# Four roundings moved ahead of the last diagonal, and one output product moved ahead of the turning of the gates

## The chip, the cores and the metric

The kernel runs on one core of a Trainium2 chip. The metric is the device time of one execution in microseconds (us). Three runs of the kernel before gave a median of 1544.88 us, from 1544.23 to 1545.69.

## The reference

A transformer layer in float32 on x of 2 x 2048 x 512 (4096 tokens): causal attention with 16 heads of 32 and rotary positions, and then a feed-forward layer with eight low-rank experts of which each token takes two. Cut to what matters:

```
def attention(x, Wq, Wk, Wv, Wo):            # x is the layernorm of the input
    q, k = rope(heads(x @ Wq.T)), rope(heads(x @ Wk.T))
    v = heads(x @ Wv.T)
    scores = where(causal, q @ k.T / sqrt(32), -inf)
    return merge(softmax(scores) @ v) @ Wo.T

def ffn(x, base_w, base_b, router_w, router_b, lora_A, lora_B):
    result = x @ base_w.T + base_b
    probs = softmax(x @ router_w.T + router_b)
    gate = top-2 of probs, made to sum to 1, zero elsewhere     # n x 8
    mid = einsum('nd,edr->ner', x, lora_A) * gate[:, :, None]
    return result + 2.0 * einsum('ner,erd->nd', mid, lora_B)

x = x + attention(layernorm(x), ...)
x = x + ffn(layernorm(x), ...)
```

## The kernel before, in words

There are three stages, each written out for every engine in its own order: `project` (queries, keys and values, with rope, into DRAM scratch), `attend` (attention) and `finish` (the output projection `Wo`, the second layernorm and the experts). An operand of a matmul is split in two: its rounded part ("hi", a cast) and the rest ("lo", the operand less its rounded part, a subtraction). A product is then hi x hi + hi x lo + lo x hi, twelve matmuls of 512 columns for one block of 128 tokens by 512.

`attend` works through 8 groups of 4 heads. In a group the four tiles of 512 queries (t = 0 to 3) take 4, 8, 12 and 16 steps, one for each 128 keys: 40 steps, done as 20 pairs, numbered 0 to 19. The last tile is pairs 12 to 19, and pairs 18 and 19 are its diagonal. For each pair TensorE (PE) makes the scores (L1014), ScalarE (ACT) the exponentials (L1114), PE the values (L1027). The sum of the exponentials is formed by adding the two steps of a pair elementwise and multiplying the result with ones on PE. In most pairs of a tile the added pair is not multiplied at once: it goes into the tile `a_gather` (two halves), either directly, or into `a_pair` and from there by an accumulating DMA of 1024 KB that GpSimd (POOL) issues (`join`, L860). Below, "join 14" is the DMA of pair 14; in the last tile pairs 14 and 16 join half 0 and pairs 15 and 17 join half 1. PE multiplies half 0 in `sums` of pair 18 and half 1 in `sums` of pair 19 (L1049), each behind a wait on all the joins of that half. Then come the later of the two steps' own columns (L1053) and `a_pair` (L1057).

`a_pair` has two places, for even and odd pairs. `wait_place_of_pair` keeps an addition from overwriting a place that a join still reads: pair 16 waits for join 14, 17 for 15, 18 for 16, and 19 for 17. ACT in turn starts a pair's exponentials only when the addition two pairs before is done.

In the last group the pairs from NO_ITEMS = 10 on are special. Row maxima (`item_max`) are over, and VectorE (DVE) does the additions (`add_pair`, L1171), which POOL does otherwise; POOL is left with the joins and with zeroing the later keys on the diagonal (`drop_later_keys`, L944). DVE also prepares the stage after it (`split_early`): the four parts of `Wo` are split (n = 0 to 3, L1156 and L1158, 128 x 512 each, from `shared` into `a_third` and `a_k_stack0`), and the first context, 128 x 2048 in `f_ctx` (`cin`), into `a_k_first` (n = 4). SP loads `f_ctx` at pair 10 (L894). When its split is done (`c_lo_done`), SP loads the second context, 1024 KB, into the same tile (L922); its next instructions are four small loads of router weights (L198), and then a wait for the last `sums`.

`finish` walks over eight tiles of 512 tokens. PE starts it with `attention_out` (L1375) for the first tile, four products, and two of the second tile, and then turns the normalised x. Its order in a tile T is in `tile`: router, down, turning of the logits, (for T > 0 two output products of the next tile,) two base products (L1435), turning of the gates (L1440), one output product of the next tile, the experts' products of two blocks (L1450), and so on. The turning waits for DVE's chain of small gate operations (`gates`, to L1633). Behind it DVE multiplies (`gate_mid`, L1638), ACT rounds (L1530), DVE subtracts (`mid_rest`, L1642), and only then can L1450 start.

The lines that set where DVE splits, and the order on PE:

```
SPLIT_FROM = NPAIR - 7
...
                    if last and p >= NO_ITEMS:
                        add_pair(g, p)
                    if last and SPLIT_FROM <= p <= SPLIT_FROM + KT:
                        split_early(p - SPLIT_FROM)
...
                base(T, u, 1)
                turn_gates(T)
                attention_out(T + 1, 1 - u, 2)
                experts(T, 0)
```

The functions that the change touches, and what calls them:

## Time and profile before

| what | value |
|---|---|
| median of 3 runs | 1544.88 us |
| the profiled execution | 1543.78 us, its span 1542.0 us |
| granted TensorE clock, mean | 0.998 |
| PE busy | 1512.4 us, 98% |
| DVE, ACT, POOL busy | 1134.3, 755.7, 890.7 us |
| HBM read and written | 96.23 and 58.72 MB |

Times in the rows are counted from the start of the span. Busy PE time is modelled, since matmuls are pipelined; starts are what is compared here. In a timeline row stand start, duration, engine, line, operation, tiles and count, and in brackets how long the engine had been idle and what released it. The chain that ended last follows the work back from the end to what released each step.

### The profile page before, as it was taken

What the parts mean: (1) busy time and instruction counts of PE and PEld (TensorE: products, weight loads), DVE (VectorE), ACT (ScalarE), POOL (GpSimd) and SP (SyncE); (2) the same over time, 40 slices, a digit from 0 to 9 for tenths busy, and PEclk for the clock granted to TensorE, in tenths of its full rate; (3) what the DMA queues carried; (4) which work ended last, traced back from release to release, by engine and by line L of the source; (5) the groups of instructions that cost most, each with busy time, mean ns of one, the idle gap of its engine ahead of it and who ended that gap; (6) DMA issues with size and microseconds to landing.
All of it is one profiled execution on the core that took longest, in us unless ns stands there. A gap on an engine that the chain in (4) does not pass through costs nothing.

```text
span 1542.0 us, 24788 instructions
## 1 busy us (share of the span) xinstructions
PE 1512.4 (98%) x9056; PEld 979.6 (64%) x9056; DVE 1134.3 (74%) x2277; ACT 755.7 (49%) x1540; POOL 890.7 (58%) x597
## 2 busy tenths in 40 slices
PE   6999999999999999999999999999999989999999
PEld 5888887745555555555555555555555537777777
DVE  6766666887877777777777877777787777666665
ACT  3222222145656656666666666665675673223221
POOL 2333232446778788788887887788887821121111
PEclk9999999999999999999999999999999999999999
DMA  6656685883476377368369359449445364222311
GB/s 205 211 188 208 204 261 188 227 189 67 90 167 149 84 158 165 84 144 186 84 138 192 83 117 203 93 97 207 99 95 127 86 145 138 82 83 95 139 67 55
DMA packets 120403, 215.83 MB, mean 140 GB/s; under 512 B 12504, under 2 KB 45784, under 8 KB 113112
## 3 DMA queue, kind: packets, MB, share of 16 engines
q1 hardware_dynamic: 102384, 136.20, 32.8%
q0 software_dynamic: 8064, 58.72, 18.6%
q10 hardware_dynamic: 9840, 19.40, 3.5%
q8 instruction: 69, 1.13, 0.3%
q14 instruction: 46, 0.38, 0.1%
HBM read 96.23 MB, written 58.72 MB: 100 GB/s over the span
## 4 chain that ended last, share of the span: by engine, by line
PE 89%; DVE 5%; DMA 3%; SPq 1%; issue 1%; ACT 1%; POOL 0%; DVEq 0%; POOLq 0%; ACTq 0%
PE a_st L1014 16%; PE a_mx L260 16%; PE a_av L1027 16%; PE p_pair L518 11%; PE f_wo_ps L1375 6%; PE f_out_ps L1435 5%; PE p_v L530 5%; PE a_sum L260 3%; PE a_sum L1049 2%; DVE a_part L275 2%; PE a_sum L1057 2%; PE f_out_ps L1450 1%; PE f_mid_ps L1375 1%; DMA a_third<-a_neg_rows 1%; PE f_tr_ps L1394 1%; DMA a_gather<-a_pair 1%
## 5 line engine op out<-in xcount | busy, mean ns | idle before, releaser
L1114 ACT ACTIVATE a_probs<-a_st 128x512 f32<-128x512 f32 (+2 forms) x1244 | 573.3, 547 | 353.9 <-PE a_st L1014 348.2
L275 DVE TENSOR_REDUCE a_part<-a_mx 128x1 f32<-128x512 f32 (+2 forms) x773 | 495.3, 681 | 90.5 <-PE a_mx L260 79.3
L963 POOL TENSOR_TENSOR a_pair<-a_probs 128x1024 f32<-128x1024 f32 (+2 forms) x224 | 401.9, 1835 | 29.8 <-issue 14.7
L963 POOL TENSOR_TENSOR a_gather<-a_probs 128x1024 f32<-128x1024 f32 x76 | 179.9, 2388 | 87.9 <-ACT a_probs L1114 87.9
L392 POOL TENSOR_TENSOR p_rot<-p_mul 128x1024 f32<-128x1024 f32 x32 | 87.5, 2735 | 193.5 <-DVE p_mul L696 193.5
L1368 POOL TENSOR_TENSOR f_x<-f_x,f_bias 128x512 f32<-128x512 f32 x32 | 40.2, 1286 | 200.2 <-DVE f_xn L1588 200.2
L1027 PE MATMUL a_av<-a_probs,shared 128*32 128x512 f32 (+3 forms) x1280 | 142.7, 546 | 0.0
L1027 PE MATMUL a_av<-a_probs,a_v 128*32 128x512 f32 (+3 forms) x1280 | 139.8, 537 | 2.2 <-POOL a_probs L944 2.2
L278 DVE CUSTOM_DVE_ANT_0 a_mx<-a_mx,f_ctx 128x512 f32<-128x512 f32 (+1 forms) x155 | 94.7, 630 | 51.4 <-PE a_mx L260 51.4
L944 POOL TENSOR_SCALAR_AFFINE_SELECT a_probs<-a_probs 128x512 f32<-128x512 f32 x128 | 88.6, 756 | 61.2 <-ACT a_probs L1114 57.3
L1014 PE MATMUL a_st<-a_q_stack,a_k_stack 98*128 98x512 f32 (+3 forms) x287 | 101.4, 371 | 1.0 <-DMA a_q_stack<-a_neg_rows 1.0
L260 PE MATMUL a_mx<-a_k_stack,a_q_stack 96*128 96x512 f32 (+3 forms) x252 | 88.0, 380 | 0.1
L604 ACT ACTIVATE p_rot_hi<-p_rot 128x1024 fp32r<-128x1024 f32 x32 | 34.0, 1061 | 110.2 <-POOL p_rot L392 94.4
L278 DVE CUSTOM_DVE_ANT_0 a_sum<-a_sum,f_ctx 128x512 f32<-128x512 f32 (+1 forms) x85 | 53.8, 633 | 29.6 <-PE a_sum L260 27.9
L700 DVE TENSOR_TENSOR p_rot_lo<-p_rot,p_rot_hi 128x1024 fp32r<-128x1024 f32 x28 | 45.7, 1633 | 36.8 <-ACT p_rot_hi L604 36.8
L518 PE MATMUL p_pair<-p_xt_lo,p_w_hi 128*128 128x512 f32 x256 | 69.9, 394 | 0.0
L1014 PE MATMUL a_st<-a_third,a_k_stack 98*128 98x512 f32 (+3 forms) x189 | 69.6, 380 | 0.1
L860 POOL DMA_DIRECT2D a_gather<-a_pair x56 | 49.2, 879 | 34.1 <-DVE a_pair L1171 18.4
L695 DVE TENSOR_TENSOR p_mul<-p_pair,p_tab 128x1024 f32<-128x1024 f32 x32 | 39.1, 1220 | 39.7 <-PE p_pair L518 39.7
L1027 PEld LDWEIGHTS a_av<-a_probs,shared 128*32 128x32 f32 x1280 | 30.5, 109 | 57.2 <-issue 42.2
L1027 PEld LDWEIGHTS a_av<-a_probs,a_v 128*32 128x32 f32 x1280 | 30.3, 108 | 57.1 <-issue 39.6
L1014 PEld LDWEIGHTS a_st<-a_q_stack,a_k_stack 98*128 98x128 f32 x287 | 54.0, 189 | 18.9 <-ACT a_probs L1114 9.7
(241 smaller groups left out, 3037.7 us busy)
## 6 DMA issues: line engine op xcount, KB each, us to landing
a_gather<-a_pair POOLq DMA_DIRECT2D x56, 1024.0 KB, 7.2
qk_scratch<-p_rot_hi SPq DMA_DIRECT2D x32, 512.0 KB, 3.1
qk_scratch<-p_rot_lo SPq DMA_DIRECT2D x32, 512.0 KB, 3.9
a_k_stack<-qk_scratch SPq DMA_DIRECT2D x60, 256.0 KB, 8.2
a_q_first<-qk_scratch SPq DMA_DIRECT2D x48, 256.0 KB, 6.9
a_third<-qk_scratch SPq DMA_DIRECT2D x36, 256.0 KB, 5.5
v_scratch<-p_v_st SPq DMA_DIRECT2D x32, 256.0 KB, 7.1
ctx_scratch<-a_ctx_st SPq DMA_DIRECT2D x32, 256.0 KB, 3.1
```

The source lines that it names most:

```text
L260: mm = pe.matmul(places[:, i, :], queries[0:96, head, qi * P:(qi + 1) * P], keys[0:96, head, 0:width], start=(i == 0), stop=not masked_her ...
L275: dve.tensor_reduce(found, scores.rearrange("p (h n) -> p h n", n=width), AX.X, ALU.max).then_inc(self.max_done, 1)
L278: dve.tensor_tensor_reduce(out=scores, in0=scores, in1=self.mask[:, TT - width:TT], scale=1.0, scalar=3.0 * MASKED, op0=ALU.add, op1=ALU.m ...
L392: pool.tensor_tensor(rot[:, par], mul[:, par, :, 0, :], mul[:, par, :, 1, :], ALU.add).then_inc(rot_done, 1)
L518: mm = pe.matmul(pair_ps[p % 2][:, half, :], w[:, kt, cols], a[u][:, kt, :], start=(n == 0), stop=(n == len(passes) - 1))
L530: mm = pe.matmul(v_ps[s % 2][:, :], a[u][:, kt, s * P:(s + 1) * P], w[:, kt, 2 * DM:3 * DM], start=(n == 0), stop=(n == len(passes) - 1))
L944: pool.affine_select(block, block, pattern=[[0, HG], [1, P]], compare_op=ALU.is_ge, fill=0.0, base=0, channel_multiplier=-1).then_inc(mask ...
L963: pool.tensor_tensor(place[:, h:h + 2, q0:TT], probs[:, s % RING, h:h + 2, q0:TT], probs[:, (s + 1) % RING, h:h + 2, q0:TT], ALU.add).then ...
L1014: pe.matmul(score_bank(g, n)[:, q0:TT], block, queries[t][0:98, h, q0:TT], start=True, stop=True).then_inc(st_done, 1)
L1027: mm = pe.matmul(av_ps[h * DK:(h + 1) * DK, q0:TT], vb[par][:, j, h * DK:(h + 1) * DK], probs[:, s % RING, h, q0:TT], start=j == 0, stop=s ...
L1114: act.activation(probs[:, s % RING, h, q0:TT], score_bank(g, HG * s + h)[:, q0:TT], ACT.Exp, scale=SCORE_SCALE).then_inc(exp_done, 1)
L1375: mm = pe.matmul(out, w, a, start=(n == 0), stop=(n == len(pairs) - 1))
```

## The change

Two edits. In the last group of `attend` the splits start at pair 10 instead of 13, and the first context is split in four parts of 128 x 512 instead of one of 128 x 2048. The parts of `Wo` go behind the additions of pairs 10 to 13, the parts of the context behind those of pairs 13 to 16, so pair 13 has two. The parts count on semaphores of their own, and behind the last part DVE waits for all four and then raises `c_hi_done` and `c_lo_done`, as the one split did. In `finish`, for the first tile only, the output product (1, block 2) stands ahead of the turning of the gates instead of behind it.

```
-SPLIT_FROM = NPAIR - 7
...
+                    m = n - KT
                     dve.wait_ge(early.ctx_loaded, 16)
-                    raw, hi, lo = early.cin, early.c_hi, early.c_lo
-                    hi_done, lo_done, count = early.c_hi_done, early.c_lo_done, 1
+                    raw, hi, lo = early.cin[:, m, :], early.c_hi[:, m, :], early.c_lo[:, m, :]
+                    hi_done, lo_done, count = early.c_part_done, early.c_rest_done, m + 1
                 dve.tensor_copy(hi, raw).then_inc(hi_done, 1)
                 dve.wait_ge(hi_done, count)
                 dve.tensor_tensor(lo, raw, hi.bitcast(F32), ALU.subtract).then_inc(lo_done, 1)
+                if n == 2 * KT - 1:
+                    dve.wait_ge(early.c_rest_done, KT)
+                    dve.sem_inc(early.c_hi_done, 1)
+                    dve.sem_inc(early.c_lo_done, 1)
...
-                    if last and SPLIT_FROM <= p <= SPLIT_FROM + KT:
-                        split_early(p - SPLIT_FROM)
+                    if last and NO_ITEMS <= p < NO_ITEMS + KT:
+                        split_early(p - NO_ITEMS)
+                    if last and NO_ITEMS + KT - 1 <= p < NO_ITEMS + 2 * KT - 1:
+                        split_early(p - NO_ITEMS + 1)
...
                 base(T, u, 1)
+                if T == 0:
+                    attention_out(1, 1, 2)
                 turn_gates(T)
-                attention_out(T + 1, 1 - u, 2)
+                if T > 0:
+                    attention_out(T + 1, 1 - u, 2)
                 experts(T, 0)
```

DVE's order in the last group before, from the addition of pair 13 (the first row) to that of pair 18 (the last). `a_third` and `a_k_stack` take the parts of `Wo`, `a_k_first` the context; L1171 is an addition.

```order
L1171 TENSOR_TENSOR a_gather<-a_probs 128x1024 x2
L1156 CAST a_third<-shared 128x512
L1158 TENSOR_TENSOR a_k_stack<-shared,a_third 128x512
L1171 TENSOR_TENSOR a_pair<-a_probs 128x1024 x2
...
L1156 CAST a_third<-shared 128x512
L1158 TENSOR_TENSOR a_k_stack<-shared,a_third 128x512
L1171 TENSOR_TENSOR a_pair<-a_probs 128x1024 x2
L1156 CAST a_k_first<-f_ctx 128x2048
L1158 TENSOR_TENSOR a_k_first<-f_ctx,a_k_first 128x2048
L1171 TENSOR_TENSOR a_pair<-a_probs 128x2x384 x2
```

Now the same stretch, from the third part of `Wo` behind the addition of pair 12 on; L1175 is the addition, and the first L1175 row is pair 13.

```order
L1156 CAST a_third<-shared 128x512
L1158 TENSOR_TENSOR a_k_stack<-shared,a_third 128x512
L1131 STREAM_TRANSPOSE a_sum_t<-a_sum 128x512
L1135 RECIPROCAL a_rsum<-a_sum_t 128x16
L1140 STREAM_TRANSPOSE a_rsum_b<-a_rsum 128x512
L1175 TENSOR_TENSOR a_gather<-a_probs 128x1024 x2
L1156 CAST a_third<-shared 128x512
L1158 TENSOR_TENSOR a_k_stack<-shared,a_third 128x512
L1156 CAST a_k_first<-f_ctx 128x512
L1158 TENSOR_TENSOR a_k_first<-f_ctx,a_k_first 128x512
L1175 TENSOR_TENSOR a_pair<-a_probs 128x1024 x2
L1156 CAST a_k_first<-f_ctx 128x512
```

A split now stands ahead of the turning of tile 2's sums, which comes before the addition of pair 13, and two splits instead of one stand between the additions of pairs 13 and 14. At the other end nothing stands any more between the additions of pairs 17 and 18:

```order
L1158 TENSOR_TENSOR a_k_first<-f_ctx,a_k_first 128x512
L1175 TENSOR_TENSOR a_pair<-a_probs 128x1024 x2
L1156 CAST a_k_first<-f_ctx 128x512
L1158 TENSOR_TENSOR a_k_first<-f_ctx,a_k_first 128x512
L1175 TENSOR_TENSOR a_pair<-a_probs 128x1024 x2
L1175 TENSOR_TENSOR a_pair<-a_probs 128x2x384 x2
```

The last context part is behind the addition of pair 16 (second row), so `c_lo_done` rises ahead of the addition of pair 17 (fifth row), and SP's load of the second context with it.

PE in the first tile of `finish` before: base products, the turning of the gates, the output product, the experts' products.

```order
L1435 MATMUL f_out_ps<-f_base_lo,f_xt_hi 128x512 x4
L1435 MATMUL f_out_ps<-f_base_hi,f_xt_lo 128x512 x4
L1440 MATMUL f_lg_ps<-f_ident,f_gate_x 128x128 x4
L1375 MATMUL f_wo_ps<-a_third,a_q_first 128x512 x4
L1375 MATMUL f_wo_ps<-a_k_stack,a_q_first 128x512 x4
L1375 MATMUL f_wo_ps<-a_third,a_q_first 128x512 x4
L1450 MATMUL f_out_ps<-f_b_hi,f_mt_hi 128x512
```

And now, at the same place:

```order
L1443 MATMUL f_out_ps<-f_base_lo,f_xt_hi 128x512 x4
L1443 MATMUL f_out_ps<-f_base_hi,f_xt_lo 128x512 x4
L1383 MATMUL f_wo_ps<-a_third,a_q_first 128x512 x4
L1383 MATMUL f_wo_ps<-a_k_stack,a_q_first 128x512 x4
L1383 MATMUL f_wo_ps<-a_third,a_q_first 128x512 x4
L1448 MATMUL f_lg_ps<-f_ident,f_gate_x 128x128 x4
L1458 MATMUL f_out_ps<-f_b_hi,f_mt_hi 128x512
```

The twelve matmuls of the product have changed places with the four of the turning, and nothing stands any more between the turning and the first of the experts' products.

## Rows read from the trace of the kernel before

**Rows 1.** The page: the chain that ended last, by engine.
```profile
PE 89%; DVE 5%; DMA 3%; SPq 1%; issue 1%; ACT 1%; POOL 0%; DVEq 0%; POOLq 0%; ACTq 0%
```

**Rows 2.** The chain that ended last: start us, us, what.
```profile
1251.63 2.37 DVE a_pair L1171 x2
...
1254.29 8.28 DMA a_gather<-a_pair
```

**Rows 3.** Timeline of DVE, end of the last group: start us, us, engine, line.
```profile
1242.11 0.71 DVE L1141 STREAM_TRANSPOSE a_rsum_b<-a_rsum 128x512 f32<-128x512 f32 x1
1243.28 3.19 DVE L1171 TENSOR_TENSOR a_gather<-a_probs 128x1024 f32<-128x1024 f32 x2 [0.47 <-ACT a_probs L1114]
1246.40 0.41 DVE L1156 CAST a_third<-shared 128x512 fp32r<-128x512 f32 x1
...
1247.46 2.35 DVE L1171 TENSOR_TENSOR a_pair<-a_probs 128x1024 f32<-128x1024 f32 x2
...
1257.02 2.36 DVE L1171 TENSOR_TENSOR a_pair<-a_probs 128x1024 f32<-128x1024 f32 x2 [1.97 <-DMA a_gather<-a_pair]
...
1262.60 2.36 DVE L1171 TENSOR_TENSOR a_pair<-a_probs 128x1024 f32<-128x1024 f32 x2 [2.15 <-DMA a_gather<-a_pair]
1264.87 1.22 DVE L1156 CAST a_k_first<-f_ctx 128x2048 fp32r<-128x2048 f32 x1
...
1269.54 2.68 DVE L1171 TENSOR_TENSOR a_pair<-a_probs 128x768 f32<-128x768 f32 x2
1273.39 0.76 DVE L1171 TENSOR_TENSOR a_pair<-a_probs 128x256 f32<-128x256 f32 x2 [1.17 <-issue]
```

**Rows 4.** POOL: join 17 and the first masks of the diagonal.
```profile
1265.25 0.97 POOL L860 DMA_DIRECT2D a_gather<-a_pair  x1 [4.71 <-DVE a_pair L1171]
...
1266.22 1.24 POOL L944 TENSOR_SCALAR_AFFINE_SELECT a_probs<-a_probs 128x512 f32<-128x512 f32 x2
```

**Rows 5.** Line L860: landing of joins 14, 17, and one beside key loads.
```profile
DMA to landing us min/median/max: 6.9/6.9/6.9
...
DMA to landing us min/median/max: 8.1/8.1/8.1
...
DMA to landing us min/median/max: 9.9/9.9/9.9
...
DMA to landing us min/median/max: 6.8/7.2/11.0
```

**Rows 6.** Windows: busy us by engine, granted clock, DMA share, GB/s.
```profile
592.60:602.50 9.90, 9.90 (x77) 5.38 (x76) 7.18 (x13) 4.67 (x14) 8.14 (x8) 1.00 1.01 222
...
1251.00:1273.40 22.40, 18.30 (x144) 8.04 (x140) 16.38 (x15) 15.16 (x36) 7.69 (x7) 1.00 0.98 206
...
1264.00:1268.00 4.00, 1.76 (x17) 0.72 (x13) 3.97 (x3) 1.40 (x5) 2.56 (x4) 1.00 0.92 190
```

**Rows 7.** Timeline of PE, end of the last group.
```profile
1272.27 0.85 PE L1057 MATMUL a_sum<-a_pair,a_ones 128*32 128x384 f32 x8 [1.82 <-DVE a_pair L1171]
...
1273.59 1.04 PE L1049 MATMUL a_sum<-a_gather,a_ones 128*32 128x512 f32 x8
...
1275.00 1.21 PE L1375 MATMUL f_wo_ps<-a_third,a_k_first 128*128 128x512 f32 x4
```

**Rows 8.** SP: the load of the second context.
```profile
1269.64 0.37 SPq L922 DMA_DIRECT2D f_ctx<-ctx_scratch  x1
```

**Rows 9.** Timeline of PE, first tile of the last stage.
```profile
1304.09 1.10 PE L1435 MATMUL f_out_ps<-f_base_hi,f_xt_lo 128*128 128x512 f32 x4
1306.33 0.66 PE L1440 MATMUL f_lg_ps<-f_ident,f_gate_x 128*128 128x128 f32 x4 [1.15 <-DVE f_gate_x L1633]
...
1309.60 0.40 PE L1450 MATMUL f_out_ps<-f_b_hi,f_mt_hi 128*128 128x512 f32 x1
```

**Rows 10.** Timeline of DVE there.
```profile
1308.41 0.69 DVE L1642 TENSOR_TENSOR f_mt_lo<-f_gated_mid,f_mt_hi 128x512 fp32r<-128x512 f32 x1 [0.70 <-ACT f_mt_hi L1530]
```

**Rows 11.** The chain that ended last: the output product there.
```profile
1306.98 2.78 PE f_wo_ps L1375 x12
```

More of the change, by code:

```diff
@@ L1237, in __init__ @@
         self.c_lo_done = ctx.enter_context(nc.semaphore("f_c_lo_done"))
+        self.c_part_done = ctx.enter_context(nc.semaphore("f_c_part_done"))
+        self.c_rest_done = ctx.enter_context(nc.semaphore("f_c_rest_done"))
     def place(self):
```

## The prediction

> **What bounds the kernel now.** I read the chain by engine first [rows 1]: 89% of the span is PE, so a change off PE's path moves the time only where PE waits. Both edits stand at such places, and each is judged by PE's start behind it.
>
> The first place is the end of the last group. The timeline of PE [rows 7] shows `sums` of pair 18 waiting 1.82 us for DVE's addition, then `sums` of pair 19 (L1049) at 1273.59, and `finish` at 1275.00. DVE's timeline [rows 3] shows why the addition of pair 18 was late: the whole-context split stands from 1264.87 to 1269.54. That is the stall the new order takes away. But the reader should also see the two additions before it, at 1257.02 and 1262.60, which had waited 1.97 and 2.15 us for a DMA, and the last one, at 1273.39, after 1.17 us of idle put down to "issue". The code says what that one waits for: its place, read by join 17. Join 17 was issued at 1265.25 and landed 8.1 us later [rows 4, 5], at 1273.35. The addition began 0.04 us behind it, and L1049 of pair 19, which waits for the same join, 0.24 us behind it. So two things end this stage within 0.3 us of each other: DVE's late addition, and a row of joins.
>
> That row is a chain. The addition of pair 14 frees join 14, its landing (6.9 us, [rows 5]) the addition of pair 16, which gives join 16; the chain of waits shows the other half of it: addition of pair 15, then 8.28 us of join 15 [rows 2], then the addition of pair 17 and join 17. And the four share the same DMA engines: from 1251.0 to 1273.4 their share was 0.98 [rows 6], 206 GB/s, 4.6 MB, of which the four joins are 4.2 MB. They queue behind each other, some 5.5 us each, so a later join 14 is a later join 17.
>
> The second place is the first tile of `finish`. PE is idle 1.15 us before the turning of the gates at 1306.33 [rows 9], waiting for DVE. Behind the turning stands the output product, 2.78 us [rows 11], and the experts' products start at 1309.60 without a wait.
>
> **First edit: the splits.** The span's end moves with L1049 of pair 19, so the cost is that of join 17's landing.
>
> Removed: 4.67 us of DVE between the additions of pairs 17 and 18 (1264.87 to 1269.54, [rows 3]). Alone this would bring PE's L1057 of pair 18 forward by at most about 2 us, since the masks it also needs end at 1266.22 + 1.24 = 1267.46 [rows 4]. But L1049 of pair 19 can't start before 1273.35. Worth: 1273.59 - 1273.35 = 0.24 us at most.
>
> Added: the splits go ahead of the chain of joins. One split of 128 x 512 takes 1.06 us from start to the next start (1246.40 to 1247.46, [rows 3]); a context part has the same shape and tile types. Those of pairs 10 and 11 fall into idle time of DVE; I give them zero. That of pair 12 delays the turning back, which ended at 1242.11 + 0.71 = 1242.82, to 1243.88; the addition of pair 13 began at 1243.28 after 0.47 us of idle, so it loses 0.60. Behind pair 13 stand two splits in place of one: another 1.06. The addition of pair 14 starts 1.66 us later, say 1.7, and its row of before has no idle time ahead of it to soak that up. It ends join 14's wait, so joins 14 to 17 shift by 1.7 each: the waits of pairs 16 and 17 for a DMA (1.97 and 2.15 us) are waits for these very joins, so they are no slack. The context parts behind the additions of 14, 15 and 16 do fit into those waits (each 1.06 against 1.97 or more); behind 14 the addition of pair 15 starts about 1.2 later, which only keeps pace. Join 17 shifts to 1275.05 by this alone. Bounds: 1.0 (if POOL's slowing of the addition of pair 13, 3.19 us for two against 2.35, falls away) and 2.2.
>
> Moved: SP's load of the second context. Before, it was issued at 1269.64 [rows 8], when join 17 was nearly through. Now `c_lo_done` rises behind the addition of pair 16: 1257.02 + 1.7 + 2.36 + 1.06 = 1262.1. Join 16 has then just been issued and join 17 hasn't. All of the load's 1.05 MB passes ahead of or among the last two joins; the small router loads behind it come along. Nobody needs that data early: PE's first use of the second context lies behind four products. What it costs: a join issued at 592.6 landed after 9.9 us instead of 6.9, and in its time 222 GB/s x 9.9 us = 2.2 MB moved, 1.15 MB of it not its own [rows 5, 6]. That is 3.0 us for 1.15 MB, 2.6 us for each. In the window of before 4.6 - 4.2 = 0.4 MB of other traffic was already inside; so 0.65 MB are new, 1.7 us. Bounds: 0, if the load only takes gaps, and 3.4, from the slowest join of all, 11.0 - 6.9 = 4.1 us [rows 5], less the 0.7 that a load in join 17's way could have cost already. I take 1.7, by the row nearest in bytes.
>
> The Trainium skill speaks against the edit here too: "DMA: Bandwidth & Descriptors", section "Issuing engines are not separate DMA queues", says that transfers started by different engines run on the same 16 DMA engines and interleave. By that rule the load isn't free though SP issues it and POOL the joins; the 9.9 us of the join at 592.6 [rows 5] agree, and a reading by separate queues would put this term at 0.
>
> Sum of the first edit: join 17 lands at 1273.35 + 1.7 + 1.7 = 1276.75. L1049 of pair 19 starts at 1276.8 instead of 1273.59: **+3.2 us**. The late addition of pair 18 no longer shows: with masks and join 16 shifted it ends near 1273. The addition of pair 19 takes 0.76 and is done before PE reaches it, as before.
>
> **Second edit: the product ahead of the turning.** Counts don't change; twelve matmuls change places with four. PE's idle time ends at 1306.33 and was 1.15, so the base products ended at 1305.18 [rows 9]. Now the output product runs from there, 2.78 us, to 1307.96, and the turning starts 1.6 us later than before, though the gates were ready. By starts, four matmuls of 512 take 0.93, which puts the end of the base products at 1304.09 + 0.93 = 1305.02 and the shift at 1.5. What follows the turning is a chain over three engines, DVE, ACT, DVE, which ended at 1308.41 + 0.69 = 1309.10 [rows 10]: 2.8 us behind the turning's start. Before it lay beside the output product (which ended at 1309.60, 0.5 later), now beside nothing. The experts' products start at 1309.15 + 1.5 = 1310.65 instead of 1309.60: **+1.1 us**. The idle 1.15 us is filled, and about 2.3 us open behind the turning. Bounds: +0.7 if PE resumes sooner behind the subtraction, +1.4. Downstream each step (the additions, normalising, the next turning) hangs on this product's successors and moves along.
>
> **Sum.** +3.2 + 1.1 = +4.3 us: the profiled execution goes from 1543.78 to 1548.1; its own time lies 1.1 under the median, so the median goes from 1544.88 to 1549.2. Between `finish`'s start and the gates nothing gives time back: PE's products run in one piece there.
>
> **Rivals.**
> 1. *The load is free.* Its packets only fill gaps. For: the joins alone move about 200 GB/s, far from what loads reach. Against: the DMA share is 0.98 [rows 6]. Then +1.7 - 0.2 + 1.1 = +2.6: 1547.5.
> 2. *The joins don't carry the delay* (the other side: not slower by what can be told). If the DMA queue weren't what sets join 17, a later join 14 would be made good within the waits of pairs 16 and 17 (1.97 and 2.15 us), join 17 would land at 1273.35 or before, and L1057 of pair 18 would come up to 2.0 us sooner. It decides from the point where join 17 is not the last: all 2.0 us would reach the end if the 1.17 us of "issue" weren't its landing but DVE's own. With the second edit's +1.1 that is -0.9 at best, 1544.0, and +0.9, 1545.8, if L1049 stays. For: the view names no releaser. Against: 0.04 us between landing and start.
> 3. *The load weighs more*, because its packets and the router's all go before join 17: +3.4 in place of 1.7, +6.0 in all, 1550.9.
> 4. *PE's clock drops.* With longer stalls PE is idle for much of 1265 to 1277. In the four us from 1264 PE was busy 1.76 at a granted clock of 1.00, the upper level [rows 6], so stalls of this size didn't lower it; a product at the lower level would take twice its 2.78: up to +2.8 more, 1552.
>
> **How the numbers follow.** The forecast with its own spread has 0.55, rival 1 0.17, rival 2 0.13, rival 3 0.11, rival 4 0.04. A measurement of this kernel tells about 0.2%, 3.1 us, from no change. Over that lie 0.50 of the forecast's 0.55 (+4.3), 0.03 of rival 1 (+2.6), and rivals 3 and 4: slower 0.68. Faster by as much would need more than rival 2's best case; I give it 0.03 for what I may have overlooked, and same the other 0.29. Range: 1546.2 to 1551.4, which leaves out rivals 2 and 4 and the ends of the rest, some 2 in 10.
>
> **What would show each step.** Right: the addition of pair 14 about 1.7 us later relative to the exponentials; the second context issued 7 us earlier, near 1262; joins 16 and 17 landing after 9 us or more; PE's last wait of the stage now at L1049 of pair 19 behind a DMA, over 2 us, and the wait at L1057 of pair 18 changed into one for masks or join 16; in `finish` no wait before the turning and one of about 2.3 us before the first experts' product. Wrong: join 17 landing within 8 us of its issue with no shift of its issue, or L1049 following the values without a gap. The forecast falls if `finish` starts less than 2 us later than before, counted from the last row maximum of the group.

## The result and the profile after

The changed kernel takes 1554.12 us (median of 8 runs, 1548.06 to 1558.48), the kernel before in runs beside it 1543.91 us (8 runs, 1541.15 to 1547.81): ratio 1.0066, 95% interval 1.0046 to 1.0085. It is 10.2 us slower where +4.3 was forecast, and its 1554.1 lies 2.7 us above the range. The direction was right, the size wrong. One execution of the kernel before (1803.67 us) and one of `best` (2379.20 us) among the experiments were in a far slower state and are left out of every ratio, mean and fit below.

The profiled execution took 1555.68 us (span 1553.9, mean granted clock 0.992; before 1542.0 and 0.998). The page's chain by engine, which answers to [rows 1]:

```profile
PE 92%; DVE 4%; DMA 2%; issue 1%; ACT 1%; SPq 0%; POOL 0%; POOLq 0%; DVEq 0%; ACTq 0%
```

This page doesn't name the cause: DMA even lost a percent. It is in the last group. Timeline of DVE there (columns as in [rows 3]):

```profile
1250.63 2.35 DVE L1175 TENSOR_TENSOR a_pair<-a_probs 128x1024 f32<-128x1024 f32 x2
...
1260.17 2.36 DVE L1175 TENSOR_TENSOR a_pair<-a_probs 128x1024 f32<-128x1024 f32 x2 [2.79 <-DMA a_gather<-a_pair]
...
1266.72 2.36 DVE L1175 TENSOR_TENSOR a_pair<-a_probs 128x1024 f32<-128x1024 f32 x2 [3.13 <-DMA a_gather<-a_pair]
1272.20 1.83 DVE L1175 TENSOR_TENSOR a_pair<-a_probs 128x768 f32<-128x768 f32 x2 [3.11 <-POOL a_probs L943]
1281.01 0.76 DVE L1175 TENSOR_TENSOR a_pair<-a_probs 128x256 f32<-128x256 f32 x2 [6.99 <-DMA a_gather<-a_pair]
```

These are the additions of pairs 14, 16, 17, 18 and 19. The split is gone from between pairs 17 and 18, and the addition of pair 18 now waits for POOL's masks; but that of pair 19 waits 6.99 us for a DMA. In the timelines of POOL and SP, join 17 is issued at 1269.38 and the load of the second context at 1263.78, 5.6 us ahead of it (before, 4.4 us behind join 17: [rows 4, 8]). The first row is join 16:

```profile
1262.83 0.86 POOL L859 DMA_DIRECT2D a_gather<-a_pair  x1 [5.34 <-DVE a_pair L1175]
1269.38 0.86 POOL L859 DMA_DIRECT2D a_gather<-a_pair  x1 [5.69 <-DVE a_pair L1175]
```

```profile
1263.78 0.37 SPq L921 DMA_DIRECT2D f_ctx<-ctx_scratch  x1
```

Landing of join 17, from the view of its line; [rows 5] had 8.1:

```profile
  DVE a_pair L1175: 7.0, 1
  PEld a_sum L1048: 3.9, 1
  PE a_sum L1048: 3.6, 1
...
DMA to landing us min/median/max: 11.6/11.6/11.6
```

PE, in answer to [rows 7]:

```profile
1270.95 1.25 PE L1026 MATMUL a_av<-a_probs,a_v 128*32 128x512 f32 x8 [4.23 <-POOL a_probs L943]
...
1280.97 1.06 PE L1048 MATMUL a_sum<-a_gather,a_ones 128*32 128x512 f32 x8 [3.64 <-DMA a_gather<-a_pair]
...
1282.79 1.65 PE L1383 MATMUL f_wo_ps<-a_third,a_k_first 128*128 128x512 f32 x3
```

The wait of 1.82 us ahead of L1057 of pair 18 is gone. PE now waits 4.23 us for POOL's masks, which stand behind join 17's issue on POOL (before, 2.24 us for the same masks), and the last sums of the group wait 3.64 us for join 17. `finish` starts at 1282.79. Behind it, the place of the second edit; compare [rows 9]:

```profile
1316.76 0.60 PE L1448 MATMUL f_lg_ps<-f_ident,f_gate_x 128*128 128x128 f32 x4
1319.53 0.80 PE L1458 MATMUL f_out_ps<-f_b_hi,f_mt_hi 128*128 128x512 f32 x1 [2.17 <-DVE f_mt_lo L1653]
...
1325.35 1.08 PE L1443 MATMUL f_out_ps<-f_base_hi,f_xt_hi 128*128 128x512 f32 x4
```

The 1.15 us of idle ahead of the turning are gone, and 2.17 us stand behind it. The windows (columns as in [rows 6]) show what [rows 6] didn't have, a granted clock below 1.00 from 1270 to 1290:

```profile
1253.29:1280.98 27.69, 19.38 (x141) 8.66 (x138) 11.60 (x14) 16.74 (x36) 6.12 (x8) 0.94 0.88 191
...
1270.00:1280.00 10.00, 6.39 (x60) 2.63 (x60) 1.83 (x2) 3.69 (x8) 2.91 (x5) 0.83 0.82 197
1280.00:1290.00 10.00, 9.03 (x50) 6.70 (x51) 5.28 (x8) 0.51 (x4) 2.11 (x5) 0.83 0.48 159
```

To compare kernels I count times in the group from the start of its transposition of the negated row maxima on DVE ("the group's zero": 1228.56 before, 1229.94 after), which lies ahead of both edits. A landing is the issue plus a time given in tenths, so differences of landings are good to about 0.1 us:

| | before | after | difference |
|---|---|---|---|
| the group's zero, from the span's start | 1228.56 | 1229.94 | +1.38 |
| addition of pair 14 starts | 18.90 | 20.69 | +1.79 |
| join 17 issued | 36.69 | 39.44 | +2.75 |
| join 17 landed | 44.79 | 51.04 | +6.25 |
| first product of `finish` | 46.44 | 52.85 | +6.41 |
| first experts' product | 81.04 | 89.59 | +8.55 |
| end of the span, from the span's start | 1542.0 | 1553.9 | +11.9 |

The forecast had +3.2 in the fifth line (first product of `finish`) and +4.3 in the sixth (first experts' product).

### The profile page after: what moved, and what is told of

Same layout as the page of the kernel before. It is cut to its first block, busy times and chain, and to the rows that moved or that the text cites. A ratio compares the mean times of both kernels' runs of the same rounds, so it can differ in the third digit from the quotient of the medians.

```text
span 1553.9 us, 24796 instructions
## 1 busy us (share of the span) xinstructions
PE 1520.4 (98%) x9056; PEld 985.3 (63%) x9056; DVE 1133.3 (73%) x2283; ACT 756.3 (49%) x1540; POOL 889.4 (57%) x597
## 3 DMA queue, kind: packets, MB, share of 16 engines
q8 instruction: 69, 1.13, 0.3%
## 4 chain that ended last, share of the span: by engine, by line
PE 92%; DVE 4%; DMA 2%; issue 1%; ACT 1%; SPq 0%; POOL 0%; POOLq 0%; DVEq 0%; ACTq 0%
PE a_mx L259 17%; PE a_st L1013 16%; PE a_av L1026 16%; PE p_pair L517 11%; PE f_wo_ps L1383 6%; PE p_v L529 5%; PE f_out_ps L1443 5%; PE a_sum L259 3%; PE a_sum L1048 2%; PE a_sum L1056 2%; DVE a_part L274 2%; PE f_mid_ps L1383 1%; DMA a_gather<-a_pair 1%; PE f_out_ps L1458 1%; PE f_lg_ps L1413 1%; PE a_mx L263 1%
```

## The experiments

Twelve kernels were run, four at a time, with the kernel before beside each lot; its medians there were 1544.75, 1544.23 and 1544.98 us, and each ratio is to the lot's own. All runs of the first edit below but `best` and the repeat have `finish` as before. They were to tell apart what makes join 17 late (the later join 14, the early load, the split's place) and how much is left for the second edit and the clock.

### Each edit alone

`first_only` is the first edit with `finish` as before; `second_only` is this alone:

```
+                if T == 0:
+                    attention_out(1, 1, 2)
                 turn_gates(T)
-                attention_out(T + 1, 1 - u, 2)
+                if T > 0:
+                    attention_out(T + 1, 1 - u, 2)
```

Expected of `first_only`:

> The first edit alone (splits from pair 10, context in four parts), the output product of the first tile left behind the turning of the gates. Measured from the last row maximum of the group to the first product of the last stage, the changed kernel needed 6.4 us more than the kernel before. Theory of the joins (the splits ahead of the addition of pair 14 delay join 14, and the second context's load runs among joins 16 and 17): this stretch is again about 6.4 longer, and the median 6.5 to 8 us over the kernel before, the part over 6.4 being products at the lower clock behind the stall. Rival, that the second edit made most of the loss (its own wait of 2.2 us and the low clock behind it): under 4 us over.

Measured: 1551.85 us, ratio 1.0041 [1.0026, 1.0057]. The last sums start at 50.96 behind the group's zero, as in the kernel with both edits (51.03), and `finish` 5.96 us later than before. The theory of the joins holds, and the rival (under 4 us over) is out.

Expected of `second_only`:

> The second edit alone. By the order of the instructions: 1.0 us later from the turning of the logits to the first of the experts' products. In the changed kernel the clock was also low behind that wait, and the products there took 1.6 us more. Theory that the new wait of 2.2 us alone brings the clock down: 2.6 us over, a granted clock under 1.00 in the 12 us behind it. Rival, that the low clock there came from the first edit's stalls as well: 1.0 us over and the clock at 1.00.

Measured: 1547.36 us, ratio 1.0013 [1.0000, 1.0025]. The timeline of PE:

```profile
1297.90 1.20 PE L1435 MATMUL f_out_ps<-f_base_hi,f_xt_hi 128*128 128x512 f32 x4
...
1306.38 0.60 PE L1440 MATMUL f_lg_ps<-f_ident,f_gate_x 128*128 128x128 f32 x4
1309.14 0.50 PE L1450 MATMUL f_out_ps<-f_b_hi,f_mt_hi 128*128 128x512 f32 x1 [2.17 <-DVE f_mt_lo L1645]
```

From the first base product to the first experts' product it is 1309.14 - 1297.90 = 11.24 us, and 11.24 in the changed kernel too (1308.29 to 1319.53); before it was 10.28. The second edit costs 0.96 us by order, the same with and without the first, and 1.07 up to the next base product (15.53 against 14.46 us from the first one). The granted clock behind the wait stayed at 1.00, as the rival had it, so that wait alone didn't bring the clock down. The first edit is the larger part.

### The load held back, splits as in the change

`first_held` takes the two semaphores' rise away from behind the last split and puts it behind the addition of pair 17; `first_held19` puts it behind that of pair 19 (shown):

```
-                if n == 2 * KT - 1:
-                    dve.wait_ge(early.c_rest_done, KT)
-                    dve.sem_inc(early.c_hi_done, 1)
-                    dve.sem_inc(early.c_lo_done, 1)
...
                         add_pair(g, p)
+                    if last and p == NPAIR - 1:
+                        dve.wait_ge(early.c_rest_done, KT)
+                        dve.sem_inc(early.c_hi_done, 1)
+                        dve.sem_inc(early.c_lo_done, 1)
```

> As the first edit alone, but DVE raises the two context semaphores behind the addition of pair 17 instead of with the last part, so SP issues the second context's load where it did before; the splits still stand ahead of join 14. Theory that the early load is the larger term: join 17 lands 2 to 3 us later than in the kernel before (relative to the last row maximum), the stretch to the last stage is 2 to 3 us longer, the median 2 to 3.5 over. Rival, that the delay of the additions alone does it (join 15 issued too close behind join 14): the stretch is 5 us longer or more with the load held too.

Measured: 1553.41 us, 1.0056 [1.0034, 1.0077]. It didn't hold the load as meant: SP issued it at 36.99, while the addition of pair 17 was still running, 2.5 us before join 17's issue at 39.48. Join 17 landed at 51.08, no better than in the change (51.04). So an issue 3 us later doesn't help; only one behind join 17's could. Neither theory was tested, since the load hadn't been held. That called for the second version.

> The first edit with its own placement of the splits, and the context semaphores raised behind pair 19, so that only the delay of the additions is left. Theory of the chain (join 14 is issued 1.8 us later, join 17 2.8 later): join 17 lands 2 to 3 us later than before, near 47.3, the last stage starts 2 to 3 us later. Rival, that the joins make the delay good in the waits of pairs 16 and 17: within 0.5 us.

Measured: 1546.75 us, 1.0025 [1.0012, 1.0038]. The load is issued at 46.81, and join 17 lands at 46.51 after 7.0 us:

```profile
DMA to landing us min/median/max: 7.0/7.0/7.0
```

That is 1.72 later than before (44.79), less than the 2 to 3 expected. What is left to delay it is the place of the splits, by which the addition of pair 14 starts at 20.74 instead of 18.90. The forecast's first term was 1.7, but the steps differ: join 17 was issued 2.82 us later (39.51 against 36.69) and landed after 7.0 us instead of 8.1, so the agreement to the tenth is in part luck.

PE shows something else here. Its last sums start at 47.82 behind the group's zero, 1.3 us after join 17's landing and without a wait:

```profile
1271.75 1.20 PE L1048 MATMUL a_sum<-a_gather,a_ones 128*32 128x512 f32 x8
...
1274.29 1.03 PE L1048 MATMUL a_sum<-a_gather,a_ones 128*32 128x512 f32 x8
```

PE came late because the masks and with them the values of pair 18 were late (41.09 against 38.37), and because the granted clock from 1260 to 1270 was 0.76. `finish` starts at 49.22, 2.78 later than before.

### The splits in idle time, the load early, held, and at its old place

Here parts 0 and 1 of `Wo` go behind the addition of pair 10 and parts 2 and 3 behind that of pair 11, where DVE idles; the context's parts behind those of pairs 13 to 16:

```
-                    if last and NO_ITEMS <= p < NO_ITEMS + KT:
-                        split_early(p - NO_ITEMS)
+                    if last and NO_ITEMS <= p < NO_ITEMS + 2:
+                        split_early(2 * (p - NO_ITEMS))
+                        split_early(2 * (p - NO_ITEMS) + 1)
```

`idle_early` raises the semaphores behind the last split as the change does, the three others behind the addition of pair 17, 18 or 19. The addition of pair 14 starts at 18.87 in `idle_early`, as before (18.90), so that the delay of join 14 is out in all four, and the load, with the four small loads behind it, is what differs.

> The first edit with its splits put where DVE was idle: Wo parts 0 and 1 behind the addition of pair 10, 2 and 3 behind pair 11, the context's four parts behind pairs 13 to 16, so that the addition of pair 14 starts as early as in the kernel before; the second context's load stays early (behind pair 16). Theory that the early load is the larger term: joins 16 and 17 land after 9 us or more, and the stretch is 3 to 4.5 us longer. Rival, that the delay of the additions does it: within 1 us of the kernel before.

> The same placement in idle time, and the two context semaphores raised behind the addition of pair 17, so neither the additions nor the load move. Both theories: join 17 lands as in the kernel before or up to 0.5 us sooner, L1057 of pair 18 no longer waits 1.8 us, and the stretch is 0 to 0.5 us shorter, since join 17 sets its end; the median within 1 us of the kernel before. If instead DVE's late addition of pair 18 was the true end of the stage, and join 17 not, it is 1.5 to 2 us shorter.

> The splits in DVE's idle time, as in the two kernels before it, but the two context semaphores raised behind the addition of pair 19, which itself waits for join 17. (Behind pair 17 they were raised while that addition ran, so the second context's load had moved up by 7 us all the same.) The load now can't run beside any join. Theory that the load made joins 16 and 17 late (9.7 and 12.3 us, 4.2 us for join 17): join 17 lands 44 to 45 us behind the last row maximum's transpose, as before or up to 0.7 sooner, and the last stage starts 46 to 46.5 behind it (before: 46.4); the median within 1 us of the kernel before. Rival, that the missing split between pairs 17 and 18 or POOL's earlier masks slow the joins: join 17 lands at 48 or later again.

| | load issued | join 17 issued | join 17 landed | time us | ratio |
|---|---|---|---|---|---|
| before | 41.08 | 36.69 | 44.79 | | |
| `idle_early` | 32.01 | 36.80 | 49.30 | 1550.56 | 1.0038 [1.0023, 1.0052] |
| `idle_held` | 34.17 | 36.67 | 48.97 | 1550.91 | 1.0041 [1.0027, 1.0054] |
| `idle_held19` | 45.12 | 36.77 | 44.77 | 1546.39 | 1.0009 [0.9997, 1.0022] |

The windows from join 14's issue to join 17's landing, first `idle_held19`, then `idle_early`, give the price:

```profile
1252.26:1275.44 23.18, 19.59 (x153) 8.45 (x152) 12.13 (x14) 16.66 (x38) 6.09 (x8) 1.00 0.88 182
```

```profile
1250.25:1278.03 27.78, 21.15 (x154) 8.91 (x154) 11.71 (x14) 18.58 (x39) 5.96 (x8) 0.94 0.89 190
```

23.18 us x 182 GB/s = 4.2 MB, the four joins alone. 27.78 x 190 = 5.3 MB, the joins and the load. So 1.06 MB more go with 4.6 us more, 4.3 us per MB; the joins' own bytes take 23.18 / 4.2 = 5.5 there. The same stretch of the kernel before (1250.11 to 1273.35) moved 198 GB/s in 23.24 us, 4.6 MB. So 0.4 MB of the load went through behind join 17's issue for nothing, at a higher rate than `idle_early` reached: where the bytes stand counts, and not only how many they are.

`idle_held` missed: it was meant to leave the load where it was, but the load went out at 34.17 and join 17 landed at 48.97 instead of at 44.8. `idle_held19` is the run that both theories needed. Join 17 lands at 44.77 there, as the load theory had it; its rival, 48 or later through POOL's earlier masks or the missing split, is out. The waits of PE, of `idle_early` and `idle_held19`:

```profile
1278.02 1.81 PE L1048 MATMUL a_sum<-a_gather,a_ones 128*32 128x512 f32 x8 [4.23 <-DMA a_gather<-a_pair]
```

```profile
1275.54 1.06 PE L1048 MATMUL a_sum<-a_gather,a_ones 128*32 128x512 f32 x8 [1.09 <-DMA a_gather<-a_pair]
...
1286.25 1.20 PE L1384 MATMUL f_wo_ps<-a_third,a_k_first 128*128 128x512 f32 x4 [0.66 <-DVE f_x L1582]
```

The second row of `idle_held19` shows that a load behind everything isn't free either: `x` and the biases stand behind it on SP's queue, `finish` waits for `x` (0.66 and 0.37 us in two places), and the turning of the gates comes 33.3 us behind `finish`'s first product instead of 31.3. The kernel before had the load where it costs neither.

`idle_held18` tests this: the rise behind the addition of pair 18, the load at about its old place.

> Same placement of the splits, but the two semaphores are raised behind the addition of pair 18, so that SP issues the second context at about 41 as in the kernel before: the first edit's removal of the stall, with no delay of join 14 and no early load. Theory A (join 17 sets the end of the group): join 17 lands at 44.8, the last sums start at 44.9 to 45.0 and the first product of the last stage at 46.3, 0.0 to 0.2 before its place in the kernel before, and nothing is lost later, since the load isn't later than before; ratio 0.999 to 1.0005. Rival (the late addition of pair 18 also cost something that shows only in the time): 0.998 or less, 3 us faster.

Measured: 1543.36 us, 0.9998 [0.9987, 1.0009]. The load is issued at 40.16, join 17 lands at 44.97, and PE's rows are

```profile
1272.31 1.07 PE L1048 MATMUL a_sum<-a_gather,a_ones 128*32 128x512 f32 x8 [0.28 <-DMA a_gather<-a_pair]
...
1273.74 0.50 PE L1384 MATMUL f_wo_ps<-a_third,a_k_first 128*128 128x512 f32 x1
```

at 45.00 and 46.43 behind the group's zero; before, 45.03 and 46.44. The stall of 4.67 us on DVE is wholly gone and the end of the stage hasn't moved by more than 0.03 us. Whatever held DVE there, join 17 held PE. The rival, 3 us faster, is out.

### The small loads behind the context

Four router loads (128 x 8 each, 4 KB) go out right behind the context. `router_late` is `idle_early` with these moved:

```
+            sp.wait_ge(early.pair_done, PAIRS_DONE)
             for n in range(W_RING, 2 * W_RING):
                 weights.load(sp, n)
-            sp.wait_ge(early.pair_done, PAIRS_DONE)
```

> Splits in DVE's idle time, the second context issued early (about 32 us behind the start of the group's last transposition), as in the kernel before it with this placement, but the four small router loads (128 x 8 each) that stood right behind it on SP's queue are moved behind SP's wait for the last sums. Theory A, the 1.05 MB of the context itself is what joins 16 and 17 pay for: join 17 lands at 48.8 to 49.4 as with the router loads beside it (49.30), ratio to before 1.003 to 1.005. Theory B, the small packets of the router loads cost the joins part of it: join 17 lands at 47.5 or earlier (44.8 + 1.7 to 2.7), ratio 1.002 or less.

Measured: join 17 lands at 49.04 after 12.2 us; in `idle_early` at 49.30 after 12.5. The small loads cost about 0.3 us of it, and theory A stands on position. The time, 1553.51 us, 1.0047 [1.0027, 1.0067], isn't lower, and `finish` shows why: the load of `x` now queues behind the router's, and PE waits 2.04 us for it (0.17 in `idle_early`):

```profile
1295.44 1.58 PE L1384 MATMUL f_wo_ps<-a_third,a_q_first 128*128 128x512 f32 x4 [2.04 <-DVE f_x L1582]
```

### Both places filled in `finish`

`both_fill` keeps the idle time ahead of the turning filled and puts the next product into the one that opens behind it:

```
+                if T == 0:
+                    attention_out(1, 1, 2)
                 turn_gates(T)
-                attention_out(T + 1, 1 - u, 2)
+                if T == 0:
+                    attention_out(1, 1, 3)
+                else:
+                    attention_out(T + 1, 1 - u, 2)
                 experts(T, 0)
                 experts(T, 1)
-                attention_out(T + 1, 1 - u, 3)
+                if T > 0:
+                    attention_out(T + 1, 1 - u, 3)
```

> The kernel before, but in the first tile the output product (1, block 2) stands ahead of the turning of the gates and the product (1, block 3) behind it, where block 2 stood. Both waits are then filled: PE's 1.15 us ahead of the turning is gone and the chain DVE, ACT, DVE behind it lies beside a product again. Theory: 1.0 us less than the kernel before from the turning of the logits to the second base product of the tile, and no clock change. Rival: block 3's bank or DVE's order (its addition of block 2 comes behind the gating) makes a base product wait as long, and nothing is gained.

Measured: 1543.81 us, 0.9998 [0.9987, 1.0010]. Neither wait is left in PE's rows; from the turning on the rows join end to start:

```profile
1308.05 0.60 PE L1440 MATMUL f_lg_ps<-f_ident,f_gate_x 128*128 128x128 f32 x4
1308.40 1.17 PE L1375 MATMUL f_wo_ps<-a_third,a_q_first 128*128 128x512 f32 x4
...
1311.26 0.40 PE L1450 MATMUL f_out_ps<-f_b_hi,f_mt_hi 128*128 128x512 f32 x1
```

From the first base product to the base product behind the experts' it is 13.33 us, against 14.46 before: 1.13 by position, as expected. The times alone can't tell it from nothing. `best` joins `idle_held18` and `both_fill`:

> The kernel before with its two changes in the form that the runs so far point to: splits in idle time with the load at its old place, and in the first tile the product of block 2 ahead of the turning and that of block 3 behind it. Theory: about 0.2 us from the first and 0.8 to 1.1 us from the second, 1 us in all, ratio 0.9993, which a measurement of this kernel can hardly tell from no change. Rival: the gain in position is given back to the granted clock, ratio 1.000 to 1.001.

Measured: 1543.32 us, 0.9992 [0.9979, 1.0006]. It isn't shown to be faster than the kernel before; its median is 11 us below that of the change.

### The change again, and the clock

> The changed kernel once more, on the chip and beside the runs of the kernel before that the experiments have. Eight runs of it had a mean granted clock of 0.990 to 0.998, mean 0.9934, against 0.9958 over 35 runs of the kernel before; in each kernel a run with the clock 0.001 lower is about 0.9 us longer. Theory A (the lower clock is a consequence of the longer waits at the end): mean clock again 0.993 to 0.994, time 1553 to 1555, ratio 1.0055 to 1.007. Theory B (the clock differed by chance or by chip): mean clock 0.995 to 0.996, time 1551 to 1552.3, ratio 1.0045 to 1.005, which is the parts' sum of order alone, about +7.

Measured: 1554.97 us (6 runs, 1552.79 to 1556.89), 1.0072 [1.0055, 1.0088]; mean granted clock 0.9915. The slower time and the lower clock both come again, the clock even below theory A's 0.993 to 0.994; theory B's 0.995 to 0.996 isn't met. The profiled execution, span 1551.0, has join 17 at 51.09 behind the group's zero, as the first profile (51.04), but its first experts' product at 87.93, 1.66 earlier than there (89.59). Its slow stretch lies in the wait for join 17, where a slow PE costs nothing:

```profile
1270.00:1280.00 10.00, 7.28 (x60) 2.75 (x60) 1.83 (x2) 2.98 (x9) 3.45 (x5) 0.67 0.89 207
1280.00:1290.00 10.00, 8.72 (x56) 6.61 (x57) 6.54 (x13) 1.52 (x5) 2.12 (x5) 1.00 0.47 160
```

The clock isn't the longer waits' alone, though. `second_only`, whose last group is that of the kernel before, has

```profile
1260.00:1270.00 10.00, 7.70 (x48) 2.66 (x44) 9.59 (x6) 3.71 (x13) 5.68 (x5) 0.71 0.97 193
```

(1.00 in the profile of the kernel before) and stays at 1.00 behind its own wait of 2.17 us. Of the fourteen profiles twelve have a ten-us window below 1.00 between 1260 and 1290; only `before` and `idle_held19` have none. In `second_only` and `both_fill`, with the old last group, PE then came to the last sums 1.4 and 1.2 us behind join 17's landing, without a wait, and `finish` started at 47.70 and 47.49 instead of 46.44. In `idle_held18` and `best`, where the stall on DVE is gone, the clock was low there too (0.83 and 0.91), and `finish` started at 46.43 and 46.47. So taking the stall away may be worth about 1 us in executions with the low clock, an estimate from these four starts; the times don't show it.

To set the clock aside I put one line through time against mean clock within each of the thirteen kernels (with 84 runs of the kernel before and 14 of the change): 0.84 us per 0.001 of clock. Read off at a clock of 0.995, where no mean lies further than 0.0024 away:

| kernel | mean clock | us at 0.995 | against before |
|---|---|---|---|
| before | 0.9955 | 1544.9 | |
| the change (14 runs) | 0.9926 | 1552.4 | +7.5 |
| `first_only` | 0.9946 | 1550.7 | +5.8 |
| `first_held` | 0.9933 | 1551.6 | +6.7 |
| `idle_early` | 0.9942 | 1549.9 | +5.0 |
| `idle_held` | 0.9945 | 1550.1 | +5.2 |
| `router_late` | 0.9932 | 1551.0 | +6.0 |
| `first_held19` | 0.9955 | 1547.7 | +2.8 |
| `idle_held19` | 0.9957 | 1546.9 | +2.0 |
| `second_only` | 0.9940 | 1545.6 | +0.7 |
| `idle_held18` | 0.9962 | 1545.0 | +0.1 |
| `best` | 0.9965 | 1544.4 | -0.5 |
| `both_fill` | 0.9946 | 1543.5 | -1.4 |

Single runs scatter by about 1.3 us around the line, so a difference here has a standard error of some 0.4 us, more for the kernels with 6 to 9 runs. The line is a fit, not a measurement of its own. By it the order of the work costs 7.5 us, and the change's lower mean clock 0.0029 x 840 = 2.4 us on top: together 9.9. That this meets the measured 10.2 is no check, since the fit only divides the difference in two; whether the edits cause the lower clock is taken up below.

## Why the prediction was wrong

**The mis-sized term: the early load.** "So 0.65 MB are new, 1.7 us. Bounds: 0 ... and 3.4" was 4.5 us: join 17 landed at 49.30 with the load early and at 44.77 with it out of the way, nothing else changed. Two steps went wrong, both in the same direction. The price per byte came from a single join [rows 5, 6]: 1.15 MB for 3.0 us. (The caption there says key loads; the trace shows SP's loads of queries and stores of a context.) In the row of four a MB ahead of join 17 went with 4.3 us instead of 2.6. A lone join moves 1.05 MB in 6.9 us, 152 GB/s, the row 182 GB/s without any load, so the row may leave fewer gaps for other packets; that this is the reason isn't shown. And the 0.4 MB of the load that already lay in the window of before were subtracted as if they had been paid for; they were free, since join 17 landed at 44.79 with them and at 44.77 without. At the old price without this subtraction the term would have been 1.05 x 2.6 = 2.7; the rest, to 4.5, is the price. The upper bound of 3.4 was built on the same single joins and failed with them. Rival 3 had the direction of this but the same bound, and stopped at 1550.9.

**What held.** Join 17 sets the end of the group in the change (+6.25 at its landing, +6.41 at `finish`) and wherever the last sums wait for it, and taking the stall away with nothing else moved was worth nothing (`idle_held18`; forecast at most 0.24). It isn't so in every profile: in `first_held19`, `second_only` and `both_fill` PE came later than join 17. Rival 2 is out: without the early load join 17 still landed 1.72 late, and without the stall nothing came sooner. The delay of join 14 reaches join 17's landing: 1.7 forecast, 1.72 measured. 1.72 + 4.53 make the whole 6.25, and the load's 4.53 comes out of both pairs, 49.30 - 44.77 and 51.04 - 46.51. At equal clock the load at its early against its old place (`idle_early`, `idle_held18`) is 4.9 us of time; the place of the splits is only 0.8 in either pair (`first_only` against `idle_early`, `first_held19` against `idle_held19`), each difference with a standard error of about 0.5. SP's load cost POOL's joins 4.5 us though neither engine waits for the other, which excludes rival 1, the free load. The rule of the Trainium skill's page "DMA: Bandwidth & Descriptors", section "Issuing engines are not separate DMA queues", that such transfers interleave on the same 16 DMA engines, agrees with this. The second edit: +1.1 forecast, 0.96 by order up to the experts' products and 1.07 up to the next base product; a wait of "about 2.3 us" behind the turning, 2.17 measured.

**Rival 4 was under-priced.** It had 0.04 and the argument that a window of four us with PE 1.76 busy was at a clock of 1.00. In the first profile of the change, `finish`'s products up to the transposition took 17.97 us instead of 16.79 (+1.18), and the stretch from the first experts' product to the next base product 5.82 instead of 4.18 (+1.64, of which 0.11 is order). The second profile of the same kernel has neither: 16.66 and 4.29. The low clock isn't an alternative to the forecast but an addition to it, 2.4 us by the fit over 14 runs. That longer waits for join 17 lower the clock is suggested by the means: the six kernels in which join 17 is over 4 us late have 0.9926 to 0.9946, and the four with the load at its old place or later and `finish` as before 0.9955 to 0.9962. But `second_only` (0.9940) and `both_fill` (0.9946) have a low one with join 17 on time. And much of what the clock lacks lies where no edit reaches: taking each ten us times the share of the clock that is missing, the two profiles of the change lack 6.8 and 8.5 us between 310 and 360 and 5.2 and 3.4 behind 1250; that of the kernel before lacks 3.4 and 0, and the other eleven 0 to 8.5 and 0 to 5.6. So it isn't shown that the edits cost these 2.4 us, and the cause of the lower mean stays open.

**The profiled span, 11.9 us.** Ahead of the group's zero +1.38, with no edit there: the granted clock from 310 to 430 us was 0.94 against 0.97 before. In the group +6.25, `finish`'s start +0.16 more at the low clock. In `finish` +1.18 by clock and +0.96 by order, then +1.53 by clock and +0.11 by order, and about 0.3 that I can't place.

Had the load been priced at 4.5, the same sum would have read -0.2 + 1.7 + 4.5 + 1.1 = +7.1, where the table at equal clock has +7.5; what the lower clock adds isn't in it.

## What to carry to other kernels

Before a wait is shortened, ask which signal rises earlier through it and what that releases: here four small splits released a 1 MB load into a row of transfers that ended the stage. Ask whether bytes that enter a row of transfers go ahead of its last one or behind it, price them in that row and not by a lone transfer, and don't count bytes as paid that had run in the row's tail. An idle stretch filled on one side of a short chain opens on the other, unless there is work for both.

## What the runs showed of the hardware that wasn't expected

- A load of 1.05 MB issued anywhere from 4.8 to 2.5 us ahead of a join cost it nearly the same (`idle_early` and `idle_held`): landings at 49.30 and 48.97. Issued 3.4 us behind the join (`idle_held18`), it cost 0.2 us.
- A semaphore raised by DVE behind an addition, with only a wait for earlier work ahead of it, rose while the addition ran: in `idle_held` the addition of pair 17 started at 34.01 and the load was on its way at 34.17, though the addition takes 2.36 us. What must follow an operation has to wait for that operation's own semaphore.
- The addition of pair 18 ran 2.68 us before and 1.83 with the wide split gone from ahead of it in `idle_held18` (2.26 in `idle_held19`), and POOL's last two masks, 2.46 and 1.02 us in `second_only` with the split on DVE beside them, 0.64 and 0.79 in `idle_held18`. What in DVE's order makes the difference wasn't tested, and in `idle_held18` none of it reached the end.
- The same program, with the same order, had mean granted clocks of 0.990 to 0.998 within 8 runs, and its times follow, 10 us apart.
